# A decoder block with sorted experts on one core: the row table is cleared by eight early transfers from ScalarE's queue instead of 16 padding transfers from SyncE's

## The chip, the cores and the metric

The kernel runs on one core of a Trainium2 chip. The metric is device time in microseconds (us) of one execution; the three runs of the kernel before gave 286.7, 285.6 and 286.87 us, median 286.7.

A core has five engines that run their own instruction streams and meet at semaphores: TensorE (PE, matrix products), VectorE (DVE), ScalarE (ACT), GpSimd (POOL) and SyncE (SP, which here only issues transfers and reads registers). ACT can issue transfers too, and POOL issues indirect ones, whose rows are chosen by an index. All transfers run on the same 16 DMA engines.

## The reference

A post-norm decoder layer for 32 x 64 = 2048 tokens of width 128, cut to its skeleton:

```
x = layernorm(x + self_attention(x))          # 16 heads, masked chunks
x = layernorm(x + cross_attention(x, ctx))    # softmax over heads
weights = softmax(x @ gW + gb)                # 15 experts
topv, topi = top_k(weights, 3)
gated = sum over the three of one_hot(topi) * topv
routed = einsum(expert_e(x), gated)           # expert: gelu(x W1 + b1) W2 + b2, 256 wide
shared = gelu(x sW1 + sb1) sW2 + sb2          # 512 wide
x = layernorm(shared + routed + x)
```

## The kernel before

Each engine's stream is written out by hand, in order; waits are on semaphores by name. The work runs in three stretches.

*Attention.* Self attention goes by 16 groups g (four of them a chunk c) through `scores`, `row_max`, `exps`, `row_sum`, `turn`, `weighted` and `out_proj`; cross attention by 16 pairs p through `scores2`, `head_max`, `exps2`, `head_sum`, `normalise2`, `weighted2`. The first layer's rows are stored to `x1_scr` in HBM and loaded back in another order (L428, L434), and POOL adds a bias to them in `x1_biased` (L1969).

*Routing.* For four chunks of tokens, DVE and PE pick three experts for each token (`route_top`, `ranks`, `route_slots`), and POOL scatters each token's row (128 values, its gate and its destination) into the table `x_srt` in HBM: 48 scatters (L1986), the first ones already between the pairs of cross attention, 12 for each chunk. An expert has room for 2176 rows in the table (ROOM = 2048 + 128), so the table has 15 x 2176 + 128 = 32768 rows of 130 floats, 17.04 MB.

*Tiles.* A table of 62 tiles of 128 sorted rows is made by DVE from the experts' row counts (L1757 to L1795), while PE computes the shared expert for all tokens (`shared_in` L763, `shared_out` L778 and L783). SP then loads tile after tile from `x_srt` (L475, eight buffers), PE turns it (L977) and multiplies it with its expert's weights (L985, L994), ACT does the gelu and the gate (L1319, L1327), and POOL scatters the results to `y_tok` (L2047). SP loads them back token by token, DVE sums them, and the last norm follows.

A tile that ends in the middle of its 128 rows reads rows that no token wrote. So 128 rows behind each expert's last row are set to zero from a zero tile `pad`: SP waits until the last counts are known (`s_ends`), reads 15 end rows from SBUF into registers and issues 15 transfers, after one for the last 128 rows of the table. Behind them in SP's stream stand eight register reads of `t_late` (which of the first eight tiles must wait for the last chunk's scatters, L459), and the waits for the tile table, for the 16 paddings (`s_filled`) and for the first 36 scatters; then come the tile loads. Behind the first eight loads stand eight reads of `t_landed` (L454). The experts' weights, 4.37 MB, come in one transfer (L439), which waits for the last use of the SBUF room below them.

Of the kernel before, what the change touches and what calls it, by code (L numbers as in the profile page):

```python
# [26 lines left out]
I32 = mybir.dt.int32  # L27
# [5 lines left out]
P = 128  # L33
# [4 lines left out]
NC = 4  # L38
# [22 lines left out]
NE = 15  # L61
FE = 256
NX = NE + 2
TOPK = 3
EW = FE + 2 * E + 2
ROOM = T + P
# [7 lines left out]
NS = 5  # L74
XW = E + 2
ROWS = NE * ROOM + P

K_IOTA, K_BASE, K_T, K_TP, K_J = 0, NE, 2 * NE, 2 * NE + TABLE, 2 * NE + 2 * TABLE
K_L = K_J + T // P
# [5 lines left out]
def build(nc, x_t, x_n, ctx_k, ctx_v, w_pack, c_pack, b_row, e_w, e_b2, g_w, g_b, k_row, dst_rows, out):  # L85
    v_scr = nc.dram_tensor("v_scr", [T, E], F32).ap()
    x1_scr = nc.dram_tensor("x1_scr", [T, E], F32).ap()
    x_srt = nc.dram_tensor("x_srt", [ROWS, XW], F32).ap()
    y_tok = nc.dram_tensor("y_tok", [NT * P + TOPK * T, E], F32).ap()

    with ExitStack() as ctx:
        def sb(name, shape, dt=F32):
            return ctx.enter_context(nc.sbuf_tensor(name, shape, dt))

        def sem(name):
            return ctx.enter_context(nc.semaphore(name))
# [43 lines left out]
        result_rows = sb("result_rows", [P, NG * TOPK + TABLE], I32)  # L140
        tri = sb("tri", [P, P], BF16)
        ones = sb("ones", [P, P], BF16)
        pad = sb("pad", [P, XW])
        route_in = sb("route_in", [P, 4, NE + 8])
        route_exp = sb("route_exp", [P, 4, NE + TOPK])
        chosen = sb("chosen", [P, NG, NE], BF16)
# [1 line left out]
        carry = sb("carry", [P, NC + 1, NE], BF16)  # L148
        y_rows = sb("y_rows", [P, TABLE], I32)
        slot = sb("slot", [P, NG * TOPK], mybir.dt.uint32)  # L150
        ends = sb("ends", [P, NE], I32)
        totals = sb("totals", [P, NL, NE])
        more_sum = sb("more_sum", [P, NL + 1, NE])
        run_end = sb("run_end", [P, NL, NE])
# [27 lines left out]
        gates = probs[:, 1, 0:NG * (NE + 1)].rearrange("p (g e) -> p g e", g=NG)  # L182
        ctx_room = expert_w[:, 0:6, 0:512]
        ctx_row, kT, v_turned = ctx_room[:, 0:2, :], ctx_room[:, 2:4, :], ctx_room[:, 4:6, :]
        x1T_room = xT
        x1T_out = x1T_room.rearrange("p (o l c t n) -> p c n l t o", o=OCT, l=4, c=NC, t=16, n=2)
        q_heads2 = q_heads_room.rearrange("p (a b h) -> p a b h", a=2, h=4)
# [88 lines left out]
        s_selected = sem("s_selected")  # L276
        s_payload_gates = sem("s_payload_gates")
        s_payloads = sem("s_payloads")
        s_scattered = sem("s_scattered")
        s_ends = sem("s_ends")  # L280
        s_filled = sem("s_filled")
# [99 lines left out]
        def _(sp):  # L381
# [54 lines left out]
                                 ).then_inc(s_x1_loaded[c], 16)  # L436
            sp.wait_ge(s_k_heads2, OCT)
            sp.wait_ge(s_v_pairs, OCT)
            sp.dma_start(expert_w[:, :, :], e_w.rearrange("x p f -> p x f")).then_inc(s_expert_w, 16)  # L439

            sp.wait_ge(s_out_psum, NP)
            sp.dma_start(b2_blocks, e_b2.rearrange("p (h a) -> p h a", h=2)).then_inc(s_b2, 16)
            sp.wait_ge(s_router_ready, 5)
            sp.dma_start(x_srt[NE * ROOM:ROWS, :], pad[:, :]).then_inc(s_filled, 16)
            sp.wait_ge(s_ends, 1)
            for e in range(0, NE, 4):
                k = min(4, NE - e)
                ends_of = nc.values_load_multi_w_load_instructions(
                    ends[0:1, e:e + k], engines=[SP], min_val=0, max_val=NE * ROOM - P,
                    skip_runtime_bounds_check_because="an expert has room for every token")[1]  # L450
                for j in range(k):
                    sp.dma_start(x_srt[bass.ds(ends_of[j], P), :], pad[:, :]).then_inc(s_filled, 16)
            def landed_by(n, least):
                return [sp.value_load(t_landed[0:1, n, k:k + 1], min_val=16 * (least // NB), max_val=16 * (TABLE // NB))  # L454
                        for k in range(NB)]
# [2 lines left out]
            sp.wait_ge(s_late, 1)  # L458
            rows_of = [sp.value_load(t_late[0:1, k:k + 1], min_val=16, max_val=late_rows) for k in range(NB)]  # L459
            sp.wait_ge(s_tables, 1)  # L460
            sp.wait_ge(s_filled, 16 * (NE + 1))
            sp.wait_ge(s_scattered, 16 * (SOON - 1))
            for t in range(NT):
                if t % 4 == 0:
# [44 lines left out]
        def _(pe):  # L509
# [256 lines left out]
            def shared_out(c, j):  # L766
                if j == 0:
                    pe.wait_ge(s_h_shared, 4 * c + 4)
                    pe.wait_ge(s_gatesT, c // 2 + 1)
                    if c == 0:  # L770
                        pe.wait_ge(s_b2, 16)
                    if c == 1:
                        pe.wait_ge(s_acc, 1)
                    if c == 2:
                        pe.wait_ge(s_selected, NC - 1)
                    if c == NC - 1:
                        pe.wait_ge(s_ends, 2)
                    pe.matmul(bank[SHARED_BANK[c]][:, :], gatesT[:, c // 2, :], b2_blocks[:, c % 2, :], start=True, stop=False,  # L778
                              skip_group_check=True)
                o = bank[SHARED_BANK[c]][:, E * j:E * j + E]  # L780
                for k in range(2 * c, 2 * c + 2):
                    for a in range(2):
                        mm = pe.matmul(o, h_shared[c % 2][:, k % 2, a, P * j:P * j + P],  # L783
                                       expert_w[:, NE + k % 2, FE + E * a:FE + E * a + E], start=False,
                                       stop=(k % 2 == 1 and a == 1), skip_group_check=True)
                if j == 3:
                    mm.then_inc(s_shared_out, 1)
# [208 lines left out]
                mm.then_inc(s_tile_out, 1)  # L996

            pe.wait_ge(s_h_shared, 4 * NC)
            pe.wait_ge(s_ends, 2)
            pe.wait_ge(s_slots, NC)  # L1000
            for i in range(NT + 2):
                if i < NT:
# [13 lines left out]
        def _(act):  # L1016
# [21 lines left out]
            def k_masked(c):  # L1038
                act.wait_ge(s_k_proj, c + 1)
                if c >= 2:  # L1040
                    act.wait_ge(s_scores, 4 * (c - 1))
                for h in range(4):
                    a = act.activation(k_heads[:, c % 2, h, :], bank[1][:, :], ACT.Identity, bias=bias_k_masked[:, h:h + 1],
                                       scale=m_h4[:, h:h + 1])
                a.then_inc(s_k_heads, 1)

            def exps(g):
                act.wait_ge(s_shifted, g + 1)
                if g >= 3:
                    act.wait_ge(s_probs_turned, g - 2)  # L1050
                act.activation(probs[:, g % 3, :], bank[2 + g % 2][:, :], ACT.Exp, scale=SCALE1).then_inc(s_exps, 1)
# [30 lines left out]
            def k_masked2(o):  # L1082
                act.wait_ge(s_ctx_turned, 2 * o + 1)
                for r in range(2):
                    a = act.activation(k_heads2[:, r, o, :].rearrange("p (m i j) -> p m i j", m=8, i=4),
                                       kT[:, o % 2, :].rearrange("p (j i m) -> p m i j", j=16, i=4), ACT.Copy,
                                       scale=m_par[:, r:r + 1])
                a.then_inc(s_k_heads2, 1)
# [115 lines left out]
            exps(9)  # L1204
            exps(10)
            k_masked(3)
            exps(11)
            u_out(6)
            u_out(7)
# [15 lines left out]
            x1T_by_octet(2)  # L1225
            x1T_by_octet(3)
            k_masked2(2)
            q_masked_first(slice(0, 2))
            q_masked_first(slice(2, 8))
            v_apart(2)  # L1230
# [110 lines left out]
        def _(dve):  # L1341
# [9 lines left out]
            dve.memset(run_over[:, RUNS + 1:RUNS + 2], 0.0)  # L1351
            dve.memset(run_data[:, 0, RUNS:RUNS + 1], float(NE * ROOM))
            dve.memset(tile_data[:, :], 0.0)
            dve.memset(pad[:, :], 0.0).then_inc(s_router_ready, 1)
            dve.tensor_copy(tri[:, :], consts[:, C_TRI:C_TRI + P]).then_inc(s_router_ready, 1)


# [233 lines left out]
            def router_ready():  # L1591
                dve.memset(gates[:, :, NE:NE + 1], 1.0).then_inc(s_router_ready, 1)
                dve.wait_ge(s_small, 64)
                dve.tensor_copy(run_data[:, 1, :], row_consts[:, K_RUN:K_END])
                dve.tensor_scalar(carry[:, 0, :], row_consts[:, K_BASE:K_BASE + NE], 1.0 / P, None, ALU.mult).then_inc(s_router_ready, 1)
                dve.wait_ge(s_head_psum, NG)
                dve.tensor_copy(payloads[:, :, :, E + 1].bitcast(I32),
                                result_rows[:, 0:NG * TOPK].rearrange("p (g k) -> p g k", k=TOPK)).then_inc(s_router_ready, 1)
                dve.wait_ge(s_router_ready, 5)

            def shared_result(c):
                dve.wait_ge(s_shared_out, c + 1)
# [151 lines left out]

            count_bank = bank[CHAIN_BANK[3]]
            so_far = count_bank[:, 64:64 + NC * NE].rearrange("p (c e) -> p c e", c=NC)
            dve.tensor_copy(ends[:, :], so_far[:, NC - 1, :]).then_inc(s_ends, 1)  # L1757
            dve.tensor_tensor(totals[:, 0, :], so_far[:, NC - 2, :], row_consts[:, K_FIRST:K_FIRST + NE], ALU.is_ge)
            dve.tensor_tensor(totals[:, 2:NL, :], so_far, row_consts[:, K_BASE:K_BASE + NE].unsqueeze(1).broadcast_to([P, NC, NE]),
                              ALU.subtract).then_inc(s_ends, 1)  # L1760
            shared_result(0)
            dve.wait_ge(s_ends, 2)
            NJ = T // P - 1
            by_level = table_room[:, 0:NC * NE * NJ].rearrange("p (r j) -> p r j", j=NJ)
            by_expert = table_room.rearrange("p (c e j) -> p c e j", c=NL, j=NE)
# [172 lines left out]
        def _(pool):  # L1938
            pool.memset(v_blocks[:, B // 4:B, :].rearrange("p b e -> p (b e)"), 0.0).then_inc(s_v_zero, 1)
            pool.memset(minus_half[:, :], -0.5)  # L1940

            def x_biased(c):
                if c == 0:
# [32 lines left out]
            def scatter(first, count):  # L1976

                for n in range(first, first + count):
                    g, k = n // TOPK, n % TOPK
                    if n % 12 == 0:  # L1980
                        pool.wait_ge(s_slots, g // 4 + 1)
                        pool.wait_ge(s_payload_gates, g // 4 + 1)
                        pool.wait_ge(s_payloads, 2 * (g // 4) + 2)
                    if n == SOON:
                        pool.wait_ge(s_late_rows, 16)
                    pool.indirect_dma_start(out=x_srt, out_offset=bass.IndirectOffsetOnAxis(  # L1986
                        ap=slot[:, n:n + 1], axis=0), in_=payloads[:, g, k, :], in_offset=None).then_inc(s_scattered if 1 <= n < SOON else s_late_rows, 16)
# [130 lines left out]
```

## Time and profile before

| | |
|---|---|
| runs of the kernel, median (lowest to highest) | 286.7 us (285.6 to 286.87) |
| profiled execution: span from first to last instruction | 319.6 us |
| mean granted TensorE clock in the profiled execution | 0.936 |
| busy in the profiled execution: PE, DVE, ACT, POOL | 241.1, 221.6, 192.2, 179.0 us |
| moved by DMA in the profiled execution | 31.89 MB, of which 11.47 MB written to HBM |

The profiled execution's own time is its span of 319.6 us, to which the profile adds nothing before or after; it is 32.9 us over the median of the runs. Times in rows are us from the span's start. "Idle before" in brackets is time that an engine stood idle ahead of an instruction and what ended it; "issue" and "remote" mean that the profile shows nothing that it waited for.

### The profile page before, as it was taken

The page shows a single profiled execution, that of the slowest core. Times are in us where ns is not written, and L with a number is a line of the kernel's source. Part 1 is how long each engine was busy: PE and PEld are TensorE (multiplying, and loading weights), DVE is VectorE, ACT ScalarE, POOL GpSimd, SP SyncE. Part 2 cuts the span into 40 slices and gives each one's busy share as a digit, 9 for nine tenths or more (in the row PEclk, how much of TensorE's full clock was granted, in tenths as well). Part 3 has the DMA queues.
Part 4 walks back from the last instruction along what each step waited for, and adds up shares of the span by engine and source line. Part 5 has one row for each costly group of instructions (what it writes and reads, how often), then busy time and mean ns, then how long its engine had stood idle before and what let it go on. Part 6 is the DMA issues. An engine that isn't in the chain of part 4 may idle for free.

```text
span 319.6 us, 7117 instructions
## 1 busy us (share of the span) xinstructions
PE 241.1 (75%) x2283; PEld 179.8 (56%) x2283; DVE 221.6 (69%) x630; ACT 192.2 (60%) x423; POOL 179.0 (56%) x166
## 2 busy tenths in 40 slices
PE   6989989877988767996761299688868867785970
PEld 3676868655535434452451156586857757674960
DVE  6777999989999998998520497043444434856875
ACT  4697997549976976754470350344554546563665
POOL 6132755330666738985677467135656566665752
PEclk9999999999997998998978589799999999999778
DMA  7672830124000002952211133123132263354462
GB/s 218 217 213 46 181 128 2 37 67 133 2 0 2 0 4 62 378 215 49 86 58 50 44 101 108 41 61 101 53 99 76 75 187 90 91 168 123 150 185 90
DMA packets 38597, 31.89 MB, mean 100 GB/s; under 512 B 12864, under 2 KB 31552, under 8 KB 38432
## 3 DMA queue, kind: packets, MB, share of 16 engines
q1 hardware_dynamic: 34608, 23.90, 26.6%
q0 software_dynamic: 3520, 7.27, 6.7%
q8 instruction: 19, 0.31, 0.4%
q10 hardware_dynamic: 432, 0.27, 0.3%
q14 instruction: 18, 0.15, 0.2%
HBM read 19.95 MB, written 11.47 MB: 98 GB/s over the span
## 4 chain that ended last, share of the span: by engine, by line
PE 44%; DVE 27%; issue 14%; ACT 4%; another core or an unknown queue 4%; POOL 4%; DMA 1%; DVEq 0%; SPq 0%; ACTq 0%
PE psum L994 12%; PE psum L985 9%; PE psum L783 5%; DVE prob_sums L1496 4%; PE psum L763 4%; DVE maxes L1490 3%; PE psum L977 2%; PE psum L568 2%; DVE prob_sums L1410 2%; POOL x_srt L1986 2%; PE psum L585 1%; DMA xT<-x_t 1%; DVE turned_room L1421 1%; DVE maxes L1405 1%
## 5 line engine op out<-in xcount | busy, mean ns | idle before, releaser
L2047 POOL DMA_INDIRECT y_tok<-k_heads,y_rows x62 | 62.7, 1012 | 50.8 <-ACT k_heads L1327 34.4
L1319 ACT ACTIVATE k_heads<-psum,k_heads 128x128 f32<-128x128 f32 x124 | 38.7, 365 | 38.5 <-PE psum L985 33.6
L1986 POOL DMA_INDIRECT x_srt<-v_blocks,slot x48 | 48.0, 1000 | 21.3 <-issue 17.2
L994 PE MATMUL psum<-k_heads 128*128 128x128 f32 x248 | 42.4, 295 | 18.0 <-issue 12.1
L1823 DVE COPY k_heads<-psum 128x128 f32<-128x128 f32 x62 | 17.8, 289 | 48.9 <-PE psum L977 32.7
L994 PEld LDWEIGHTS psum<-k_heads 128*128 128x128 f32 x248 | 34.2, 200 | 21.9 <-issue 15.2
L985 PE MATMUL psum<-k_heads 128*128 128x128 f32 x248 | 40.6, 288 | 5.2 <-DVE k_heads L1823 4.2
L1963 POOL TENSOR_TENSOR k_heads<-k_heads,inv_sums 128x1024 f32<-128x1024 f32 x14 | 27.1, 1939 | 24.0 <-DVE inv_sums L1503 23.9
L985 PEld LDWEIGHTS psum<-k_heads 128*128 128x128 f32 x248 | 33.8, 198 | 8.5 <-DVE k_heads L1823 7.4
L1951 POOL TENSOR_TENSOR probs<-probs,inv_sums 128x512 f32<-128x512 f32 x16 | 16.8, 1050 | 28.9 <-DVE inv_sums L1415 28.7
L1327 ACT ACTIVATE k_heads<-psum,k_heads 128x128 f32<-128x128 f32 x62 | 22.9, 370 | 11.3 <-PE psum L994 9.1
L1807 DVE COPY k_heads<-expert_w 128x514 f32 x62 | 26.8, 438 | 3.6 <-issue 2.6
L686 PE MATMUL psum<-k_heads,v_pairs 128*32 128x128 f32 x256 | 17.4, 403 | 8.0 <-POOL k_heads L1963 5.1
L662 PE MATMUL psum<-q_heads,k_heads 64*64 64x256 f32 x256 | 18.9, 412 | 3.1 <-ACT k_heads L1120 1.6
L1120 ACT ACTIVATE k_heads<-psum 128x1024 f32<-128x1024 f32 x16 | 16.3, 1022 | 8.0 <-PE psum L670 8.0
L1496 DVE TENSOR_REDUCE prob_sums<-k_heads 128x64 f32<-128x1024 f32 x16 | 19.1, 1196 | 0.5 <-issue 0.5
L568 PE MATMUL psum<-k_heads,q_heads 128*128 128x128 f32 x128 | 17.5, 281 | 2.6 <-issue 0.9
L568 PEld LDWEIGHTS psum<-k_heads,q_heads 128*128 128x128 f32 x128 | 16.1, 194 | 4.9 <-issue 4.7
L1490 DVE TENSOR_REDUCE maxes<-psum 128x64 bf16<-128x1024 f32 x16 | 18.8, 1189 | 0.0
L763 PE MATMUL psum<-ctxT_k,expert_w 128*128 128x512 f32 x32 | 17.4, 688 | 0.3 <-issue 0.3
L977 PE MATMUL psum<-consts,k_heads 128*128 128x128 f32 x62 | 17.1, 278 | 0.0
L686 PEld LDWEIGHTS psum<-k_heads,v_pairs 128*32 128x32 f32 x256 | 7.7, 119 | 16.0 <-POOL k_heads L1963 7.9
(191 smaller groups left out, 530.1 us busy)
## 6 DMA issues: line engine op xcount, KB each, us to landing
expert_w<-e_w SPq DMA_DIRECT2D x1, 4369.0 KB
k_heads<-x_srt SPq DMA_DIRECT2D x62, 65.0 KB
q_heads<-y_tok SPq DMA_DIRECT2D x8, 256.0 KB
x_srt<-pad SPq DMA_DIRECT2D x16, 65.0 KB
xT<-x_t SPq DMA_DIRECT2D x4, 256.0 KB, 5.1
ctxT_k<-ctx_k SPq DMA_DIRECT2D x2, 512.0 KB, 5.5
v_scr<-v_rows SPq DMA_DIRECT2D x4, 256.0 KB, 2.8
ctxT_v<-ctx_v SPq DMA_DIRECT2D x2, 512.0 KB, 5.0
```

The source lines that it names most:

```text
L568: mm = pe.matmul(bank[2 + g % 2][:, 128 * b:128 * b + 128], q_heads[:, c % 2, 4 * j + b, :], k_heads[:, c % 2, :, o:o + 32], start=(b == 0 ...
L686: mm = pe.matmul(bank[6 + p % 2][32 * q:32 * q + 32, 128 * b:128 * b + 128], v_pairs[:, p, j, :, :].rearrange("p a b -> p (a b)"), pr[:, : ...
L763: pe.matmul(shared_bank(k, a), expert_w[:, NE + h, P * a:P * a + P], x2T[:, 512 * c:512 * c + 512], start=True, stop=True).then_inc(s_shar ...
L985: mm = pe.matmul(bank[2 + t % 2][:, P * a:P * a + P], tile_weights(t)[:, P * a:P * a + P], x_tileT[:, t % 2, :], start=True, stop=True)
L994: mm = pe.matmul(bank[6 + t % 2][:, 0:E], h_tile[:, t % 2, a, :], tile_weights(t)[:, FE + E * a:FE + E * a + E], start=(a == 0), stop=(a = ...
L1319: ins = act.activation(h_tile[:, t % 2, a, :], bank[2 + t % 2][:, P * a:P * a + P], ACT.Gelu, bias=tile_weights(t)[:, EW - 2 + a:EW - 1 + a])
L1490: dve.tensor_reduce(maxes2[:, p % 2, :], psum[:, 1024 * (p % 2):1024 * (p % 2) + 1024].rearrange("p (g t x) -> p t g x", g=4, x=4), mybir. ...
L1496: dve.tensor_reduce(prob_sums2[:, p % 2, :], probs2[:, p % 3, :].rearrange("p (t h) -> p t h", t=B), AX_X, ALU.add).then_inc(s_inv_sums2, 1)
L1807: dve.tensor_copy(stage[:, t % NS, :], expert_w[:, bass.ds(expert_of[t % 4], 1), :].rearrange("p a b -> p (a b)")).then_inc(s_staged, 1)
L1963: pool.tensor_tensor(probs2[:, p % 3, :].rearrange("p (t h) -> p t h", t=B), probs2[:, p % 3, :].rearrange("p (t h) -> p t h", t=B), inv_s ...
L1986: pool.indirect_dma_start(out=x_srt, out_offset=bass.IndirectOffsetOnAxis(ap=slot[:, n:n + 1], axis=0), in_=payloads[:, g, k, :], in_offse ...
L2047: pool.indirect_dma_start(out=y_tok, out_offset=bass.IndirectOffsetOnAxis(ap=y_rows[:, t:t + 1].bitcast(mybir.dt.uint32), axis=0), in_=y_t ...
```

## The change

The table is set to zero as a whole, and early. POOL zeroes a piece of 128 x 260 floats in the SBUF room of the last expert's weights (`zeros`). ACT issues eight transfers from that piece, each 2.13 MB with the piece repeated 16 times in each partition: four behind `k_masked(3)` in self attention, four behind `k_masked2(2)` before cross attention. The padding, the read of the end rows, the tiles `pad` and `ends`, and DVE's two instructions for them go. SP's load of the expert weights and POOL's first scatter wait for all eight.

```diff
+Z = 2 * XW
+FILLS = 8
...
-        pad = sb("pad", [P, XW])
-        ends = sb("ends", [P, NE], I32)
+        zeros = expert_w[:, NX - 1, 0:Z]
...
+            sp.wait_ge(s_filled, 16 * FILLS)
             sp.dma_start(expert_w[:, :, :], e_w.rearrange("x p f -> p x f")).then_inc(s_expert_w, 16)
...
-            sp.wait_ge(s_router_ready, 5)
-            sp.dma_start(x_srt[NE * ROOM:ROWS, :], pad[:, :]).then_inc(s_filled, 16)
-            sp.wait_ge(s_ends, 1)
-            for e in range(0, NE, 4):
-                k = min(4, NE - e)
-                ends_of = nc.values_load_multi_w_load_instructions(
-                    ends[0:1, e:e + k], engines=[SP], min_val=0, max_val=NE * ROOM - P,
-                    skip_runtime_bounds_check_because="an expert has room for every token")[1]
-                for j in range(k):
-                    sp.dma_start(x_srt[bass.ds(ends_of[j], P), :], pad[:, :]).then_inc(s_filled, 16)
...
-            sp.wait_ge(s_filled, 16 * (NE + 1))
             sp.wait_ge(s_scattered, 16 * (SOON - 1))
...
+            def rows_cleared(first, count):
+                act.wait_ge(s_zeros, 1)
+                for i in range(first, first + count):
+                    n = ROWS * XW // P // Z
+                    part = x_srt.rearrange("(p r q) e -> p r (q e)", p=P, q=2)
+                    part = part[:, i * n // FILLS:(i + 1) * n // FILLS, :]
+                    act.dma_start(part, zeros.unsqueeze(1).broadcast_to([P, part.shape[1], Z])).then_inc(s_filled, 16)
...
             k_masked(3)
+            rows_cleared(0, 4)
             exps(11)
...
             k_masked2(2)
+            rows_cleared(4, 4)
             q_masked_first(slice(0, 2))
...
-            dve.memset(pad[:, :], 0.0).then_inc(s_router_ready, 1)
...
-            dve.tensor_copy(ends[:, :], so_far[:, NC - 1, :]).then_inc(s_ends, 1)
...
+            pool.memset(zeros, 0.0).then_inc(s_zeros, 1)
...
+                    if n == 0:
+                        pool.wait_ge(s_filled, 16 * FILLS)
```

On ACT, in self attention, the first four transfers stand between the four masked copies of the keys (L1043 before, L1035 now) and the exponentials of group 11. Before:

```order
L1051 ACTIVATE probs<-psum 128x512 x2
L1043 ACTIVATE k_heads<-psum,bias_k_masked,consts 128x512 x4
L1051 ACTIVATE probs<-psum 128x512
L1057 ACTIVATE turned_room<-psum,consts 128x128 x2
L1051 ACTIVATE probs<-psum 128x512
```

And now, in the same place of ACT's stream:

```order
L1051 ACTIVATE probs<-psum 128x512 x2
L1035 ACTIVATE k_heads<-psum,bias_k_masked,consts 128x512 x4
L1045 DMA x_srt<-expert_w 128x16x260 x4
L1051 ACTIVATE probs<-psum 128x512
L1057 ACTIVATE turned_room<-psum,consts 128x128 x2
```

The second four stand in the same way between L1085's two masked copies and the first masked queries of cross attention (L1112), so both times ACT's next activation is queued behind four issues.

On SP, behind the load of the shared expert's second bias (`v_pairs<-e_b`), the stream before went through the padding to the reads of `t_late`; the fence begins at the weights and ends in the third padding:

```order
L439 DMA expert_w<-e_w 128x17x514 [waits s_v_pairs,s_k_heads2]
L442 DMA v_pairs<-e_b 128x1024 [waits s_out_psum]
L444 DMA x_srt<-pad 128x130 [waits s_router_ready]
L448 TENSOR_LOAD ends [waits s_ends]
L452 ISA
L452 DMA x_srt<-pad 128x130
L452 ISA
```

Now SP goes from that load straight to the reads of `t_late`, and the load of the weights has one more wait:

```order
L442 DMA expert_w<-e_w 128x17x514 [waits s_filled,s_v_pairs,s_k_heads2]
L445 DMA v_pairs<-e_b 128x1024 [waits s_out_psum]
L452 TENSOR_LOAD t_late [waits s_late]
L452 ISA x2
L452 TENSOR_LOAD t_late
L452 ISA x2
```

The 16 transfers, the four reads of `ends` and their register instructions are gone from between them; what follows is unchanged.

## Rows read from the trace of the kernel before

**Rows 1.** The page: span, and the chain that ended last by engine.

```profile
span 319.6 us, 7117 instructions
...
PE 44%; DVE 27%; issue 14%; ACT 4%; another core or an unknown queue 4%; POOL 4%; DMA 1%; DVEq 0%; SPq 0%; ACTq 0%
```

**Rows 2.** That chain in order of time, 176 to 212 us: start, duration, what.

```profile
179.98 0.07 PE psum L743
...
184.97 6.08 PE psum L763 x12
191.05 0.86 PE psum L778 x2
191.91 3.57 PE psum L783 x32
...
195.59 3.44 PE psum L763 x8
199.02 3.69 issue
202.72 1.10 PE psum L778 x2
203.81 5.20 PE psum L783 x32
209.01 0.12 PE psum L977
```

**Rows 3.** Timeline of SP's issues (start, duration, line, count), whole span and 205 to 216.

```profile
71.96 3.94 SPq L434 DMA_DIRECT2D x_rows<-x_scr  x8
125.80 0.37 SPq L439 DMA_DIRECT2D expert_w<-e_w  x1
...
185.56 12.27 SPq L452 DMA_DIRECT2D x_srt<-pad  x15
205.17 10.30 SPq L475 DMA_DIRECT2D k_heads<-x_srt  x9
```

**Rows 4.** Line L459: count, ns min/median/max, first and last start.

```profile
L459 SPq TENSOR_LOAD <-t_late x8: 12/266/706, 197.8 to 204.0; - x8
L459 SPq FUSED_REGOPS  x8: 15/147/707, 197.9 to 204.3; - x8
```

**Rows 5.** Timeline of DVE around the counts, 176 to 200 us.

```profile
184.67 0.17 DVE L1757 CAST ends<-psum 128x15 int32<-128x15 f32 x1
...
192.04 0.16 DVE L1779 TENSOR_SCALAR t_late<-used_f 1x8 int32<-1x8 f32 x1
```

**Rows 6.** The page: DMA issues, KB each and median us to landing.

```profile
v_blocks<-v_scr SPq DMA_DIRECT2D x16, 64.0 KB, 2.5
...
x_rows<-x_scr SPq DMA_DIRECT2D x8, 128.0 KB, 3.0
```

**Rows 7.** Timelines around ACT's first four new issues.

```profile
45.19 2.78 ACT L1043 ACTIVATE k_heads<-psum,bias_k_masked,consts 128x512 f32<-128x512 f32 x4
48.11 0.60 ACT L1051 ACTIVATE probs<-psum 128x512 f32<-128x512 f32 x1
...
49.13 0.63 DVE L1410 TENSOR_REDUCE prob_sums<-probs 128x16 f32<-128x512 f32 x1
...
64.95 0.69 DVE L1430 TENSOR_TENSOR x_pre<-psum,x_rows 128x512 f32<-128x512 f32 x1 [0.59 <-PE psum L597]
```

**Rows 8.** Timeline around ACT's second four new issues.

```profile
73.38 2.77 ACT L1112 ACTIVATE q_heads<-v_blocks,consts 128x128 f32<-128x128 f32 x4 [0.36 <-DVE v_blocks L1465]
...
76.49 2.35 DVE L1490 TENSOR_REDUCE maxes<-psum 128x64 bf16<-128x1024 f32 x2
```

**Rows 9.** Timeline of POOL: the first use of the reloaded rows, and the first scatter.

```profile
83.70 1.31 POOL L1969 TENSOR_TENSOR x_rows<-x_rows,bias_rows 128x512 f32<-128x512 f32 x1
...
118.42 1.20 POOL L1986 DMA_INDIRECT x_srt<-v_blocks,slot  x1 [1.16 <-issue]
```

**Rows 10.** Busy by engine in the stretch of the weights' load; last: clock, DMA share, GB/s.

```profile
128.00:136.00 8.00, 7.13 (x93) 3.27 (x92) 7.85 (x10) 6.17 (x14) 7.51 (x6) 1.00 1.01 382
```

More of the change, by code:

```diff
@@ L278, in build @@
         s_payloads = sem("s_payloads")
+        s_zeros = sem("s_zeros")
         s_scattered = sem("s_scattered")
@@ L776, in shared_out @@
                     if c == NC - 1:
-                        pe.wait_ge(s_ends, 2)
+                        pe.wait_ge(s_ends, 1)
                     pe.matmul(bank[SHARED_BANK[c]][:, :], gatesT[:, c // 2, :], b2_blocks[:, c % 2, :], start=True, stop=False,
@@ L998, in _ @@
             pe.wait_ge(s_h_shared, 4 * NC)
-            pe.wait_ge(s_ends, 2)
+            pe.wait_ge(s_ends, 1)
             pe.wait_ge(s_slots, NC)
@@ L1598, in router_ready @@
                                 result_rows[:, 0:NG * TOPK].rearrange("p (g k) -> p g k", k=TOPK)).then_inc(s_router_ready, 1)
-                dve.wait_ge(s_router_ready, 5)
+                dve.wait_ge(s_router_ready, 4)
             def shared_result(c):
@@ L1761, in _ @@
             shared_result(0)
-            dve.wait_ge(s_ends, 2)
+            dve.wait_ge(s_ends, 1)
             NJ = T // P - 1
```

## The prediction

> **What bounds the kernel now.** I read the chain that ended last first, because the change takes work from one queue and puts it on another, and only work on that chain is worth its full duration. By engine [rows 1], PE holds 44% of the chain, DVE 27%, "issue" 14%, and SP's queue, where the 16 padding transfers are issued, rounds to 0%. So the padding is not what the end waits for, at least in this execution. The same chain in order of time shows why [rows 2]: from 184.97 us on, PE works through the shared expert (L763, L778, L783) without a wait for SP, and at 209.01 it turns the first sorted tile (L977). The reader is to see that the step ahead of L977 is PE's own L783 and not a transfer.
>
> Then I read how close SP comes to being that step. SP issues the 15 paddings from 185.56 to 197.83 [rows 3], then its eight reads of `t_late` stand from 197.8 on [rows 4], and its first tile load goes out at 205.17 [rows 3]. Loads of 64 KB and 128 KB land 2.5 and 3.0 us after their issue in the median [rows 6]; a tile load has 65 KB, so it lands at 207.7 to 208.2. PE comes to it at 209.01. SP is early by 0.8 to 1.3 us. That is the margin on which this prediction turns.
>
> The profiled execution took 319.6 us and the runs 286.7, so 32.9 us in it are not in the runs. The rows show where some of it lies: an "issue" of 3.69 us in PE's chain, 32 matmuls of L783 in 5.20 us where the same 32 took 3.57 [rows 2], and a padding at 12.27 / 15 = 0.82 us where eight plain issues took 3.94, 0.49 each [rows 3]. Both sides of the margin shrink when these go, so I worked it out once more without them. PE: 209.01 - 3.69 - (5.20 - 3.57) = 203.7; with the twelve L763 at the pace of the eight (3.44 / 8 x 12 = 5.16 for 6.08) and L778 at 0.86 for 1.10, 202.5. SP: 185.56 + 15 x 0.49 = 192.9, three more reads of `ends` at about the 0.27 + 0.15 of a read of `t_late` [rows 4] make 194.2, eight reads of `t_late` at the same price (3.3) make 197.5, up to 1 us more for the read of the tile's row and the waits between, and 2.5 to 3.0 for landing: 200.0 to 201.5. Again PE is last, now by 1.0 to 3.7 us. Both are estimates from these rows; the margin is small beside what I had to guess.
>
> **What is removed.** On SP: 16 issues, four reads of `ends`, and the wait until the paddings have landed. In the trace the reads of `t_late` could start when DVE has written it, 192.04 + 0.16 = 192.20 [rows 5], instead of at 197.83: 5.6 us earlier on SP. Without the pauses it is 194.2 - 192.2 = 2.0 us. This is the cap on what SP can give; under it lies PE's shared expert, which hides all of it if the margin above is right. If that cover is gone, the cap is 2.0 us less what PE then waits for anyway. The eight later loads add a second place: nine loads are issued over 10.30 us [rows 3], with the eight reads of `t_landed` ahead of the ninth, so that the ninth could be late for PE even where the first is not; the same 2.0 us caps it. I take 0.3 for both, since SP is early at the first tile by either count. On DVE the copy to `ends` (0.17 us at 184.67) [rows 5] goes from the stretch that leads to the tile table: 0.1 gained at most; the clearing of `pad` lies at the start, beside loads.
>
> **What is added on ACT.** Four issues twice. An issue costs 0.37 us for one transfer of 4.37 MB, more than twice a fill's size, to 0.49 [rows 3], so four cost 1.5 to 2.0 us. First place: the masked keys end at 45.19 + 2.78 = 47.97, the exponentials of group 11 run 48.11 to 48.71, and DVE sums them at 49.13 [rows 7], 0.42 later. If the issues start only when the keys are done, the exponentials come 1.5 to 2.0 later, of which 0.14 + 0.42 = 0.56 is free: 0.9 to 1.4 us late for DVE. DVE's next idle time that gives slack back is 0.59 at 64.95, where it waits for PE [rows 7]. If ACT's queue takes the issues while the activations before them still run, nothing is late. So 0 to 1.4; I take 0.2, nearer to nothing, because later groups have slack of their own. Second place: ACT is idle for 0.36 before the masked queries at 73.38, and DVE's maxima start at 76.49 behind them [rows 8], after 73.38 + 2.77 = 76.15; so 2.0 - 0.36 - 0.34 = 1.3 at most, 0 at least; I take 0.1. POOL's clearing of 128 x 260 values is at the start, before POOL has anything to wait for.
>
> **What the fills do to other transfers.** 17.04 MB move. The nearest stretch of heavy traffic, the load of the expert weights, moved 382 GB/s with the DMA engines full [rows 10]; at that rate the fills need 44.6 us, 22.3 for four. The first four would run from about 48 to 70, the second from 73 to 95. POOL's first scatter, which now waits for them, stands at 118.42 [rows 9], and the weights' load, which waits too, at 125.80 [rows 3]: margins of 23 and 31 us. The wait costs nothing unless the fills are slower than 17.04 MB / (118.42 - 47.97) = 242 GB/s. Eight loads of the first layer's rows are issued in the middle of it, at 71.96 to 75.90 [rows 3], and land in 3.0 us when alone [rows 6]; POOL adds their bias at 83.70 [rows 9]. Shared evenly they take about 6, landing at 82 at the latest. No cost.
>
> The sum: 0.3 + 0.1 gained, 0.2 + 0.1 lost, 0.1 us gained. Against the profiled 319.6 that is 319.5; against the median of the runs, 286.6.
>
> **The rivals.** *A, faster: without the pauses the tile loads are what PE waits for.* Speaking for it: the margin is 1 us in 209, and the estimate without pauses leans on reads of which the slowest took 0.71 us, not 0.27 [rows 4]; eight at 0.71 alone use up 3.5 us, which is the margin. Against it: the chain as recorded. It gives 2.0 + 0.1, with a bit more at the ninth load, less 0.3: about 284.5.
>
> *B, slower: ACT is held at its issues.* If an issue ends only when the descriptors of earlier transfers have drained, then each of the three fills behind the first holds ACT for one fill, 2.13 MB at 382 GB/s = 5.6 us, so 17 us per place with the exponentials queued behind: 286.6 + 17 to + 34, 304 to 321. It decides from the second issue on. Against it: 4.37 MB went out in 0.37 us [rows 3], so the size of one transfer does not hold its issuer; no row shows several big ones behind each other on one queue. The Trainium skill, "Perfetto Trace Analysis", section "DMA Instruction — HWDGE (DVE, Sync)", says that an issuing engine stays busy until the descriptors of its transfer are all generated, and that the DMA engines start early when the descriptor buffer is full. By that rule the issuer would be held by fills with many descriptors, and the time would be this rival's 304 or above. The 0.37 us of the weights' issue speak against it.
>
> *C, slower: the fills run late.* At 200 GB/s they need 85 us from 47.97, end at 133, and POOL's first scatter, with the second half of cross attention's POOL work behind it, is 14 us late: about 301. Speaking for it: the fills' packets are short rows, and 382 GB/s was seen only for the weights [rows 10].
>
> *D, slower: the loads of the first layer's rows stand behind the fills.* If the DMA engines finish what ACT queued first, the rows land at about 97 instead of before 83.70, and cross attention starts 13 us late: about 300. The Trainium skill, "DMA: Bandwidth & Descriptors", section "Queues, rings and completion order", has each DMA engine go in turn between the queues that have work, a packet at a time; that speaks against D, and no row of before shows it.
>
> *E, slightly slower:* both of ACT's delays come out at their upper ends, 1.4 + 1.3, while SP's gain stays hidden: 289.
>
> **How the numbers follow.** About 0.5%, 1.43 us, is what a measurement of this kernel can tell from no change. Forecast, no difference: 0.50, with its own range of 285.3 to 288.0. A: 0.28. B: 0.08. C: 0.05. D: 0.04. E: 0.05. The predicted time is the forecast's, 286.6. The range takes in the forecast, A and E, from 284.4 to 289.0, and leaves out B, C and D (0.17). Faster 0.28, the same 0.50, slower 0.22.
>
> **What would show it.** In the changed kernel's profile: ACT's eight issues at about 0.4 to 0.5 us each (B wrong), and the exponentials behind them on time or up to 1.4 us late; the fills all landed by about 95 to 115, and POOL's first scatter still released by its own payload and not by a fill (C wrong); the bias on the reloaded rows near 84 (D wrong); SP's first tile load several us before PE comes to it, with L783 still ahead of the first L977 in the chain. The forecast is wrong if PE's first turns came to follow SP's loads at an earlier time than before (A), or if any stretch of attention grew by more than 1.4 us.

## The result, and the profile after

The changed kernel takes 323.75 us in the median of four runs (321.92 to 324.12), the kernel before 286.15 (285.28 to 286.87): a ratio of 1.133, with a 95% interval from 1.126 to 1.141. The forecast of no difference was wrong by 37 us. Rival B, that ACT is held at its issues, is what happened: an issue ends late, and the engine's next instruction is queued behind it. Ratios here and below leave out runs over 1.5% above the fastest of the same kernel; these are six of the twelve runs of e7 below, whose median of all runs, 287.25 us against 285.44 before, is 0.6% up where its ratio is 0.999.

The page of the changed kernel: its span, the chain that ended last by engine, and two kinds of transfer with KB of each and median us from issue to landing.

```profile
span 322.3 us, 7073 instructions
...
PE 33%; DVE 26%; ACTq 11%; issue 11%; POOL 5%; DMA 5%; ACT 3%; SPq 2%; DVEq 1%; POOLq 0%
...
x_srt<-expert_w ACTq DMA_DIRECT2D x8, 2080.0 KB, 23.0
...
x_rows<-x_scr SPq DMA_DIRECT2D x8, 128.0 KB, 10.8
```

Where the chain before had nothing of ACT's queue [rows 1], it now has 11% of the span. The timeline of ACT around the two places where it issues fills (start, duration, line, operation, and in brackets the idle time of the engine before):

```profile
44.48 0.40 ACTq L1045 DMA_DIRECT2D x_srt<-expert_w  x1
...
44.91 2.05 ACTq L1045 DMA_DIRECT2D x_srt<-expert_w  x1
...
46.99 16.17 ACTq L1045 DMA_DIRECT2D x_srt<-expert_w  x2
63.27 0.60 ACT L1051 ACTIVATE probs<-psum 128x512 f32<-128x512 f32 x1 [15.71 <-issue]
...
89.70 1.19 ACT L1085 ACTIVATE k_heads<-expert_w,consts 128x512 f32<-128x512 f32 x1
89.70 2.38 ACTq L1045 DMA_DIRECT2D x_srt<-expert_w  x2
...
92.11 18.16 ACTq L1045 DMA_DIRECT2D x_srt<-expert_w  x2
110.31 0.53 ACT L1112 ACTIVATE q_heads<-v_blocks,consts 128x128 f32<-128x128 f32 x1 [18.31 <-issue]
```

The first issue of a place takes 0.40 us and the second about 2, as ACT's earlier work still runs. The third and fourth take 16.17 us together, at the second place 18.16. The activation queued behind them, which had followed at once or after 0.36 us [rows 7, 8], comes after 15.71 and 18.31 us in which ACT is idle. The same in the chain that ended last, for the last issues of each place, with two stops between the places and POOL's first scatter:

```profile
55.37 7.79 ACTq L1045
...
70.98 1.45 issue
...
77.77 2.26 issue
...
92.11 9.71 ACTq L1045
101.85 8.41 ACTq L1045
...
156.14 1.20 POOL x_srt L1989
```

What the engines did in the two holds (busy by engine; last the granted clock, the busy share of the DMA engines and GB/s):

```profile
47.50:63.00 15.50, 1.29 (x11) 1.09 (x9) 1.27 (x3) 0.06 (x1) 1.05 (x1) 0.69 1.12 273
92.50:110.30 17.80, 1.58 (x15) 1.39 (x13) 4.02 (x9) 0.00 (x0) 0.00 (x0) 0.65 1.11 283
```

Nearly everything stands still but the DMA engines, which are full at 273 and 283 GB/s. The mean granted clock is 0.69 and 0.65 of 2.4 GHz: with PE busy for 1.29 and 1.58 us of these stretches, it fell to its lower level, 1.2 GHz, within them.

### The profile page after: what moved, and what is told of

It reads as the page before. It is cut to its first block, busy times and chain, and to the rows that moved or that the text cites. A ratio compares the mean times of both kernels' runs of the same rounds, so it can differ in the third digit from the quotient of the medians.

```text
span 322.3 us, 7073 instructions
## 1 busy us (share of the span) xinstructions
PE 236.3 (73%) x2283; PEld 178.7 (55%) x2283; DVE 222.0 (69%) x628; ACT 191.6 (59%) x423; POOL 178.6 (55%) x167
## 4 chain that ended last, share of the span: by engine, by line
PE 33%; DVE 26%; ACTq 11%; issue 11%; POOL 5%; DMA 5%; ACT 3%; SPq 2%; DVEq 1%; POOLq 0%
ACTq L1045 11%; DVE prob_sums L1497 4%; PE psum L977 4%; PE psum L986 4%; PE psum L755 4%; PE psum L775 4%; DVE maxes L1491 3%; PE psum L560 3%; DMA k_heads<-x_srt 2%; PE psum L577 2%; POOL x_srt L1989 2%; POOL y_tok L2050 2%; PE psum L654 2%; PE psum L589 2%; PE psum L770 2%
## 5 line engine op out<-in xcount | busy, mean ns | idle before, releaser
L2050 POOL DMA_INDIRECT y_tok<-k_heads,y_rows x62 | 61.9, 999 | 20.2 <-issue 12.2
L977 PE MATMUL psum<-k_heads 128*128 128x128 f32 x248 | 40.0, 286 | 3.6 <-DVE k_heads L1823 3.6
L986 PE MATMUL psum<-k_heads 128*128 128x128 f32 x248 | 39.4, 283 | 0.9 <-ACT k_heads L1321 0.9
L654 PE MATMUL psum<-q_heads,k_heads 64*64 64x256 f32 x256 | 20.6, 446 | 19.5 <-ACT q_heads L1112 17.2
L654 PEld LDWEIGHTS psum<-q_heads,k_heads 64*64 64x64 f32 x256 | 9.7, 149 | 27.9 <-ACT q_heads L1112 18.0
L1051 ACT ACTIVATE probs<-psum 128x512 f32<-128x512 f32 x16 | 9.5, 603 | 22.4 <-issue 15.7
L1411 DVE TENSOR_REDUCE prob_sums<-probs 128x16 f32<-128x512 f32 x16 | 10.7, 669 | 15.9 <-ACT probs L1051 15.8
L560 PE MATMUL psum<-k_heads,q_heads 128*128 128x128 f32 x128 | 18.5, 292 | 2.1 <-issue 0.9
L560 PEld LDWEIGHTS psum<-k_heads,q_heads 128*128 128x128 f32 x128 | 17.1, 204 | 4.4 <-issue 4.2
```

Source lines behind the costliest of these rows:

```text
L560: mm = pe.matmul(bank[2 + g % 2][:, 128 * b:128 * b + 128], q_heads[:, c % 2, 4 * j + b, :], k_heads[:, c % 2, :, o:o + 32], start=(b == 0 ...
L654: mm = pe.matmul(bank[2 * (p % 2) + a][64 * n:64 * n + 64, 256 * r:256 * r + 256], k_heads2[64 * a:64 * a + 64, r, o, cols], q_heads2[64 * ...
L977: mm = pe.matmul(bank[2 + t % 2][:, P * a:P * a + P], tile_weights(t)[:, P * a:P * a + P], x_tileT[:, t % 2, :], start=True, stop=True)
L986: mm = pe.matmul(bank[6 + t % 2][:, 0:E], h_tile[:, t % 2, a, :], tile_weights(t)[:, FE + E * a:FE + E * a + E], start=(a == 0), stop=(a = ...
L2050: pool.indirect_dma_start(out=y_tok, out_offset=bass.IndirectOffsetOnAxis(ap=y_rows[:, t:t + 1].bitcast(mybir.dt.uint32), axis=0), in_=y_t ...
```

## The experiments

A fill is one of the eight clearing transfers, and a row of a fill is one contiguous piece that it writes: 1040 bytes in the change, two rows of the table. A queue drains as the DMA engines move its rows. Theory 1 says that ACT is held because its queue is full of the rows of earlier fills. Theory 2: the queue takes a number of transfers or of bytes. Theory 3: it is the traffic of 17 MB that slows the core, wherever it is issued. All ratios are to the kernel before on the same chip.

**e1, longer rows.** The same eight transfers at the same places, in 4096 rows of 4160 bytes instead of 16384 of 1040.

```diff
-Z = 2 * XW
+Z = 8 * XW
...
-        zeros = expert_w[:, NX - 1, 0:Z]
+        zeros = expert_w[:, NX - 3:NX, :].rearrange("p a b -> p (a b)")[:, 0:Z]
...
-                    part = x_srt.rearrange("(p r q) e -> p r (q e)", p=P, q=2)
+                    part = x_srt.rearrange("(p r q) e -> p r (q e)", p=P, q=8)
```

> The same 17.04 MB in the same eight transfers at the same two places, but from a zero piece of 128 x 1040 floats, so a fill has 512 rows of 4160 bytes instead of 2048 rows of 1040. Theory 1 (ACT is held because the two fills ahead fill its queue with about 4096 descriptors): four fills are 2048 descriptors, no issue is held, each takes 0.4 to 0.5 us as the first two did, and the time is 284 to 288 us. Theory 2 (the queue holds two transfers, or about 4.3 MB): the third and fourth issue are held for 8 us each as before, 318 to 324 us. Theory 3 (it is the traffic of the fills that slows the core, not the issue): 310 to 324 us whatever the issues take.

292.46 us, 1.028 times before (1.022 to 1.034), above the 284 to 288 of theory 1 and far below theories 2 and 3. ACT's issues, then its next activation:

```profile
43.02 0.41 ACTq L1045 DMA_DIRECT2D x_srt<-expert_w  x1
43.45 0.53 ACTq L1045 DMA_DIRECT2D x_srt<-expert_w  x1
44.01 1.20 ACTq L1045 DMA_DIRECT2D x_srt<-expert_w  x1
45.24 2.32 ACTq L1045 DMA_DIRECT2D x_srt<-expert_w  x1
47.66 0.60 ACT L1051 ACTIVATE probs<-psum 128x512 f32<-128x512 f32 x1 [1.57 <-issue]
```

Four transfers of the same bytes go out in 4.5 us instead of 18.6. So neither the number of transfers nor the bytes hold ACT for 8 us; the rows do. Theory 2 is out. But the third and fourth are not as quick as the first, and 6.6 us are still lost. Part of it is a new wait on DVE:

```profile
68.34 0.69 DVE L1431 TENSOR_TENSOR x_pre<-psum,x_rows 128x512 f32<-128x512 f32 x1 [2.77 <-DMA x_scr<-x_pre]
```

DVE's buffer `x_pre` comes free only when SP's store of it has landed. In the kernel before that store had no one waiting for it; now the slowest lands 12.6 us after its issue.

**e2, the padding kept.** The kernel before with its padding, plus the fills of e1 on a semaphore of their own, `s_cleared`.

```diff
+            sp.wait_ge(s_cleared, 16 * FILLS)
             sp.dma_start(expert_w[:, :, :], e_w.rearrange("x p f -> p x f")).then_inc(s_expert_w, 16)
...
             k_masked(3)
+            rows_cleared(0, 4)
             exps(11)
...
             k_masked2(2)
+            rows_cleared(4, 4)
             q_masked_first(slice(0, 2))
```

> The kernel before with all its padding kept, and the wide fills of the run above added to it. If the removed padding was hidden under PE's shared expert, it takes the same time as that run within 1.4 us. If the padding was on the path, it is 1.5 to 2.5 us slower than that run. Against the kernel before it gives the cost of the fills alone: 0 to 2 us under theory 1, some 35 us under theories 2 and 3.

291.11 us, 1.026 (1.017 to 1.034): no difference from e1. The removed padding is worth nothing that can be measured. The reason is not the one that I gave. PE's turns of tiles around the tile start, in e1 without padding:

```profile
192.09 0.38 PE L969 MATMUL psum<-consts,k_heads 128*128 128x128 f32 x2
...
204.52 0.47 PE L969 MATMUL psum<-consts,k_heads 128*128 128x128 f32 x1 [4.57 <-DMA k_heads<-x_srt]
```

Then in e2, with the padding ahead of the loads:

```profile
197.11 0.30 PE L983 MATMUL psum<-consts,k_heads 128*128 128x128 f32 x1 [1.26 <-DMA k_heads<-x_srt]
198.12 0.33 PE L983 MATMUL psum<-consts,k_heads 128*128 128x128 f32 x1 [0.71 <-DMA k_heads<-x_srt]
...
207.22 0.33 PE L983 MATMUL psum<-consts,k_heads 128*128 128x128 f32 x1 [1.82 <-DMA k_heads<-x_srt]
```

With the padding PE does wait for the first two tiles (1.26 and 0.71 us); without it, it does not. But both kernels stop at the ninth tile, whose load must wait for the last chunk's scatters. The chain that ended last goes there through the last scatter and the ninth load, in e1:

```profile
200.25 2.28 DMA x_srt<-v_blocks,slot
202.69 1.79 DMA k_heads<-x_srt
```

and in e2, whose execution runs behind that of e1 from before the padding on (1.83 us at the first store, 45.58 against 43.75):

```profile
202.51 2.71 DMA x_srt<-v_blocks,slot
205.37 1.81 DMA k_heads<-x_srt
```

What PE gains at the first tile it spends at the ninth, waiting 4.57 us instead of 1.82 for POOL's last scatter, which the padding does not touch. In the change itself the ninth tile waits 3.61 us in the same way, at 238.19.

**e3, small transfers.** The change's rows of 1040 bytes in 32 transfers of 512 rows, 16 at each place.

```diff
-FILLS = 8
+FILLS = 32
...
-            rows_cleared(0, 4)
+            rows_cleared(0, 16)
...
-            rows_cleared(4, 4)
+            rows_cleared(16, 16)
```

> The same rows of 1040 bytes, in 32 transfers of 512 rows, 16 at each place. If the queue holds two transfers, the third issue of each place is the first one held. If it holds about 4096 descriptors or 4.3 MB, eight or nine go out at 0.4 to 0.5 us each and then every one takes about 2 us. The sum of ACT's hold is about the same in both, so 318 to 326 us.

335.49 us in one run, above the 318 to 326 that I expected. ACT's issues at the first place from the third to the sixteenth, in pieces of its timeline:

```profile
45.60 1.07 ACTq L1045 DMA_DIRECT2D x_srt<-expert_w  x1
46.70 1.41 ACTq L1045 DMA_DIRECT2D x_srt<-expert_w  x1
48.14 5.64 ACTq L1045 DMA_DIRECT2D x_srt<-expert_w  x4
53.80 15.49 ACTq L1045 DMA_DIRECT2D x_srt<-expert_w  x8
```

There are two steps. The third to eighth take 1.07 to 1.41 us; from the ninth on the mean is 15.49 / 8 = 1.94, which is the time in which 532 KB move at 275 GB/s: ACT goes at the pace at which the rows drain. That step lies where theory 1 put it. The first one, at the third issue, it did not expect; behind two outstanding fills an issue is slower, but not by a drain. The run is slower than the change because ACT is idle longer, 21.73 and 25.60 us at the two places.

**e4, two at a time.** The change's fills, two at each of four places.

```diff
             v_out(2)
+            rows_cleared(0, 2)
             k_masked2(0)
...
-            rows_cleared(0, 4)
+            rows_cleared(2, 2)
...
-            rows_cleared(4, 4)
+            rows_cleared(4, 2)
...
             exps2(2)
+            rows_cleared(6, 2)
             exps2(3)
```

> The eight narrow fills as in the change, but two at a time at four places of ACT's stream (behind the third piece of v's copies, the last masked keys, the last masked context keys and the exponentials of the third pair). Two fills were never held at a place, so with theory 1 or 2 no issue takes over 2.5 us, unless the pair before has not drained, and the time is 285 to 290 us. With theory 3 it stays above 305 us.

297.74 us, 1.046 (1.035 to 1.058), outside what theory 1 expected. ACT's issues at the fourth place, and the activation behind them:

```profile
89.40 7.72 ACTq L1045 DMA_DIRECT2D x_srt<-expert_w  x2
97.22 1.02 ACT L1120 ACTIVATE k_heads<-psum 128x1024 f32<-128x1024 f32 x1 [5.69 <-issue]
```

The fourth pair came 13 us behind the third, which had not drained: 5.69 us of hold. The second fill of the other pairs is held a little too. The early pair also met SP's loads of `v_blocks`, whose last eight issues took 11.3 us instead of 4.6. This run lies below the 305 us of theory 3, but it mixes both costs and does not tell theory 1 from 2; it shows that two fills at a time do not make a place on ACT safe.

**e5, the longest rows.** As e1, with rows of 16640 bytes (`Z = 32 * XW`), 128 to a fill.

> The same eight fills at the same two places of ACT's stream, with rows of 16640 bytes: 128 rows a fill, 1024 in all. After e1 and e3 theory 1 reads: an issue ends when the descriptors of the issue before it are all in a queue that holds about 2048, at some 1.4 us for 512 while the DMA engines are busy. It then expects every issue at 0.4 to 0.6 us, four in under 2.2 us, against 4.5 with 512 rows and 18.7 with 2048. If instead the third and fourth issue are held for their place among the outstanding transfers, they take over 1 us again. The store of the first layer's rows takes turns with the fills: if a turn is a packet of the row's length, it lands 20 us or more after its issue (7 to 10 with 1040 bytes, 12.5 with 4160), and the time is 290 to 300 us; if rows are cut into smaller packets, 12 us and 290 to 293 us.

301.75 us, 1.058 (1.054 to 1.062), just above the 290 to 300 that I expected. ACT's four issues at the first place:

```profile
45.06 0.35 ACTq L1045 DMA_DIRECT2D x_srt<-expert_w  x1
45.45 1.45 ACTq L1045 DMA_DIRECT2D x_srt<-expert_w  x2
46.93 1.22 ACTq L1045 DMA_DIRECT2D x_srt<-expert_w  x1
```

3.1 us for four, less than with 512 rows, but the fourth at 1.22 is not the 0.4 to 0.6 of theory 1: a price of about 1 us stays for an issue behind two outstanding fills, whatever the rows. The time has become worse than e1's, and not by ACT. The store and the loads of the first layer's rows take turns with the fills, and the longer a row of the fills, the longer they wait, here on DVE and on POOL:

```profile
69.55 0.69 DVE L1431 TENSOR_TENSOR x_pre<-psum,x_rows 128x512 f32<-128x512 f32 x1 [6.97 <-DMA x_scr<-x_pre]
...
102.90 1.26 POOL L1970 TENSOR_TENSOR x_rows<-x_rows,bias_rows 128x512 f32<-128x512 f32 x1 [10.18 <-DMA x_rows<-x_scr]
```

The slowest store took 2.3 us to land before, 10.1 in the change, 12.6 in e1 and 23.5 here; the loads took 3.0 in the median [rows 6], then 10.8, 15.9 and 19.2. This is the wait of rival D, by taking turns and not by standing behind whole fills; it came with taking B away.

**e6, on SP.** The change's fills, issued by SP: four behind the last small load, four behind the loads of the first layer's rows.

```diff
+            rows_cleared(0, 4)
             for c in range(NC):
                 sp.wait_ge(s_x1, 4 * c + 4)
...
+            rows_cleared(4, 4)
             sp.wait_ge(s_k_heads2, OCT)
```

> The narrow fills of the change, unchanged in rows, bytes and number, but issued from SP's stream: four behind the last small load (39 us), four behind the loads of the first layer's rows. SP is held at the third and fourth as ACT was (8 us each). If the hold of ACT is what costs 37 us, at least 25 of them go, and what is left is the lateness of SP's stores and the shared traffic: 288 to 300 us. If the traffic of the fills is the cause, 315 to 325 us.

303.57 us, 1.061 (1.055 to 1.066): 20 of the 37 us are gone, fewer than theory 1 expected and far more than theory 3 allows. Most of the rest is a wait of DVE, for the store that now stood behind SP's own held issues: SP issued it at 61.42 instead of 45.22, and it landed 17.14 us later, behind the fills on its own queue.

```profile
78.78 0.69 DVE L1432 TENSOR_TENSOR x_pre<-psum,x_rows 128x512 f32<-128x512 f32 x1 [14.96 <-DMA x_scr<-x_pre]
```

So the hold goes with the fills to whichever engine issues them, and costs what is queued behind it there. The second four have nothing due behind them; e8 tries them alone.

**e7, in the gaps.** The rows of e1, two fills on SP behind the second store of the first layer's rows and six behind the loads.

```diff
                              x1_pre[:, c % 2, :, :]).then_inc(s_x1_stored[c % 2], 16)
+                if c == 1:
+                    rows_cleared(0, 2)
...
+            rows_cleared(2, 6)
             sp.wait_ge(s_k_heads2, OCT)
```

> The wide fills of e1, issued from SP where no transfer is waited for: two behind the second store of the first layer's rows, six behind the loads of these rows. If e1's 6.6 us are ACT's hold of 1.5 us at the first place and the late store of the second chunk's rows, they go, and the time is that of the kernel before within 2 us (284 to 288). If the removed padding is worth something once nothing collides, it is 1.4 to 2.5 us faster than the kernel before. If 17 MB of writes cost by themselves, it stays at 290 us or above.

The ratio is 0.999 (0.994 to 1.004). The 37 us are gone, and nothing that can be measured is gained: 17 MB of writes in rows of 4160 bytes cost nothing that shows where nobody waits for a transfer, and the padding was worth as little. SP is held here too. Of its six issues behind the loads these are the third and fourth together, then the fifth:

```profile
77.12 5.11 SPq L434 DMA_DIRECT2D x_srt<-expert_w  x2
...
82.28 5.04 SPq L434 DMA_DIRECT2D x_srt<-expert_w  x1
```

The third takes 1.29 us and the fourth 3.78. Nothing behind them on SP is due before the weights' load at 125.26.

**e8, half of the change on SP.** The change with only the second four fills moved to SP.

```diff
+            rows_cleared(4, 4)
             sp.wait_ge(s_k_heads2, OCT)
...
             k_masked2(2)
-            rows_cleared(4, 4)
```

> The change with one edit: its second four fills go out from SP, behind the loads of the first layer's rows, and the first four stay on ACT. If each place costs what ACT is held there, the 18.3 us of ACT's idle time ahead of the masked queries go and the 15.7 us of the first place stay: 304 to 308 us. If the second four cost by their traffic wherever they are issued, 318 us or above.

305.49 us, 1.071 (1.062 to 1.080), as expected: 18.3 us less than the change, so the second four cost nothing that shows when SP issues them. ACT keeps its first hold and loses the second:

```profile
63.34 0.60 ACT L1059 ACTIVATE probs<-psum 128x512 f32<-128x512 f32 x1 [15.20 <-issue]
...
92.45 2.76 ACT L1120 ACTIVATE q_heads<-v_blocks,consts 128x128 f32<-128x128 f32 x4 [1.70 <-DVE v_blocks L1473]
```

**e9, the change's rows in the gaps.** As e7 with `Z = 2 * XW`.

> The change's narrow fills (1040 bytes a row) at the places of e7 on SP's stream. SP may be held for 8 us at the third to sixth of the second group, with nothing behind that is due. By the rate of the narrow fills, 8 us each, the last of six lands at about 76 + 48 = 124, some 8 us behind the time at which POOL would scatter its first rows. If no other wait counts, the time is that of the kernel before plus 0 to 9 us, 285 to 295. If narrow rows cost by themselves, 300 us or above.

301.52 us, 1.054 (1.044 to 1.063). I had expected 285 to 295. The loads of the first layer's rows were done later, at 81 instead of 76 us, because the last stores had met the first two fills; and six fills took 51 us from there. POOL's first scatter waited for the last one:

```profile
132.25 1.20 POOL L1990 DMA_INDIRECT x_srt<-v_blocks,slot  x1 [15.02 <-DMA x_srt<-expert_w]
```

In e7 the same scatter stood at 118.74, 13.5 us earlier. This is rival C: with rows of 1040 bytes the fills are slow enough to be what the scatter waits for, once they are not begun early.

## Why the prediction was wrong

e7 is the changed kernel with nothing different but its fills (engine, places, and the length of a row), and its time is that of before. Its timelines of ACT (three activations that follow a place) and of POOL give the times against which the change's stand:

```profile
47.61 0.60 ACT L1054 ACTIVATE probs<-psum 128x512 f32<-128x512 f32 x1
...
70.18 2.31 ACT L1088 ACTIVATE k_heads<-expert_w,consts 128x512 f32<-128x512 f32 x2
74.07 2.75 ACT L1115 ACTIVATE q_heads<-v_blocks,consts 128x128 f32<-128x128 f32 x4 [1.58 <-DVE v_blocks L1467]
...
118.74 1.20 POOL L1990 DMA_INDIRECT x_srt<-v_blocks,slot  x1 [1.25 <-DVE v_blocks L1587]
```

In the change they stand at 63.27, 89.70, 110.31 and 156.14. So the first place costs 63.27 - 47.61 = 15.7 us; between the places 19.52 - 15.66 = 3.9 more are lost; the second place costs 36.24 - 19.52 = 16.7; and 1.2 follow up to the first scatter. Together 37.4, of the 39.3 by which the spans of these two executions differ (322.3 and 283.0 us; the medians of the change and of before differ by 37.6). The two places are 32.4 of them. In the 3.9 lie two stops of PE, 1.45 and 2.26 us, that the chain calls "issue"; what they wait for stays open. To the 3.9 also belongs what the hold did to the clock. One stretch behind the first hold (last the granted clock, the DMA share and GB/s), and the same four products in it and later:

```profile
63.00:67.00 4.00, 2.83 (x13) 2.66 (x13) 2.17 (x4) 1.11 (x3) 1.05 (x1) 0.50 1.10 273
...
64.17 1.22 PE L589 MATMUL psum<-weights,turned_room 128*128 128x128 f32 x4 [15.38 <-ACT turned_room L1057]
...
73.90 0.61 PE L589 MATMUL psum<-weights,turned_room 128*128 128x128 f32 x4
```

PE waited 15.38 us for ACT, and from there to 67 us the clock stood at its lower level, 1.2 GHz: the four products took 1.22 us instead of 0.61.

**The step that failed** is "An issue costs 0.37 us for one transfer of 4.37 MB, more than twice a fill's size, to 0.49 [rows 3], so four cost 1.5 to 2.0 us." Four cost 18.6 us at the first place and 20.5 at the second. The row was right and did not bear on the question: 0.37 us [rows 3] is the price of an issue on an empty queue, and the weights' load was alone on it. The first fill cost 0.40 as well. I wrote under B that no row shows several big ones behind each other on one queue, and then let the single row count against it with a chance of 0.08. Its price (17 us a place) was nearly right, for two errors that cancel: two fills of the four are held, not three, and each for some 8 us, not 5.6, since rows of 1040 bytes drain at 273 to 283 GB/s and not at the 382 of the weights [rows 10]. The rule of the Trainium skill ("Perfetto Trace Analysis", "DMA Instruction — HWDGE (DVE, Sync)"), that an issuing engine stays busy until the descriptors of its transfer are all made, would have given the right side; these traces agree with it from the second issue on (2.05 and 16.17 us), not for the first, which took 0.40 us with as many rows.

**What an issue waits for.** e1, e3, e5 and e7 separate two things. Behind two outstanding fills an issue takes 1.0 to 1.4 us (once 2.3) even with 128 rows. The number of transfers alone does not do that: before, SP's eight loads of the first layer's rows went out at 0.49 us each [rows 3], with several of them outstanding at once, since each took 3.0 us to land; beside the fills of the change they took 7.82 us.

With many rows outstanding an issue takes as long as the rows ahead take to drain. In e3 the drain sets in at the ninth issue of 512 rows, in the change at the third of 2048, in e1 and e5 (512 and 128 rows, four issues) not at all, in e7 on SP at the fourth of 512. At most 1536 rows of fills stood ahead of that one. In e5 SP's eight loads beside the fills have 256 rows each; the sixth and seventh were held for 6.47 and 7.97 us, behind at most 1280 and 1536 rows. Counted from the packets of the traces, between about 1050 and 1800 rows of the transfers ahead were still to move when a held issue ended. A limit on the rows ahead, which leaves out the transfer being handed over, fits these runs; it is not one number, and what sets it, and where the price of 1 us is from, was not tried. That the last transfer is left out fits e3 against the change: ACT is idle for 21.73 us in place of 15.71 at the first place, 6.0 more, and the 1536 rows by which the last transfers differ need 5.8 us at 275 GB/s, an estimate from the rates above.

**The margin between SP and PE.** I held PE to be last at the tile start by 1.0 to 3.7 us. In an execution without the pauses it is not: in e2, which keeps the padding, PE waited 1.26 us for the first tile. Rival A was right there. That the gain is nil all the same comes from a wait that I did not name: the ninth load stands behind the last chunk's scatters. I had the ninth load as late because of SP's register reads.

**The other terms.** The loads of the first layer's rows took 10.8 us in place of my 6, and stayed hidden in the change: POOL's bias on them, at 121.23, followed DVE and not a transfer. The rule of the Trainium skill that each DMA engine goes in turn between queues, a packet at a time ("DMA: Bandwidth & Descriptors", "Queues, rings and completion order"), agrees with the change, where the loads landed after 10.8 us and the fills queued beside them after 23.0 (medians). e1 and e5 add that the landing of a short row's transfer grows with the row of the fills. POOL's first scatter waited for no fill in the change, because the holds had made it late too; at 275 GB/s instead of 382 the fills need 62 us, so from 47.97 on the margin is 8 us and not 23 (an estimate), and e9, which issues six of them from 81 on, had none.

## What to carry to other kernels

The duration of an issue in a trace is its price on the queue as it stood then: before putting several large transfers behind each other, count the rows ahead of each and ask what is queued behind the issue on that engine. Few long rows spare the issuer and slow every transfer of short rows beside them, so bulk writes belong on an engine with nothing due and in a stretch where no store or load is waited for. And an instruction taken off a path is worth only the distance to the next thing that ends last there: with the padding in place PE already waited 1.82 us at the ninth tile for the last scatter, so an earlier first tile could gain nothing.

## What was unexpected of the hardware

The row length of a bulk write set three things at once: the rate (273 to 283 GB/s with 1040 bytes; in e7 with 4160 bytes the row below), the hold of the issuer, and the landing of other queues' transfers (a 256 KB store: 2.3 us alone, at most 10.1, 12.6 and 23.5 us beside rows of 1040, 4160 and 16640 bytes). e7, one stretch of ten us in the middle of the fills:

```profile
80.00:90.00 10.00, 9.25 (x106) 5.08 (x108) 9.90 (x13) 9.16 (x11) 5.84 (x4) 1.00 1.03 409
```

With the DMA engines full, PE, DVE and ACT are busy for 9.2 to 9.9 of ten us, and the clock stays at its higher level.
